# Attention units in four rounds in place of five, with both projections of the next unit at the front of the first round

## The chip, the cores and the metric

The kernel runs on one core of one Trainium2 chip. The metric is device time in microseconds (us). Before the change the median of three runs is 837.76 us (836.8 to 838.21).

## The reference, cut to what matters

The model is four residual blocks on x of shape (2, 1024, 128), in fp32: attention, a mixture of experts, a state space layer, and the mixture again. The change touches the attention alone:

```python
qk = layernorm(x) @ W_qk                    # 16 heads of 64, queries and keys
scores = (q * 64 ** -0.5) @ k.T, causal
out = softmax(scores) @ k                   # the keys are the values too
x = x + out @ W_out
```

Then come `x + ffn(layernorm(x))` (16 experts of width 64, the best 2, and a shared one), `x + ssm(layernorm(x))`, and the ffn again.

## The kernel before

Engines run programs of their own, written out by hand, and meet at semaphores. What each engine does next is fixed by the order of the calls in its program; no planner and no due times are involved. The attention is cut into 16 units, each one pair of heads (two heads of 64 rows, which fill 128 partitions) of one batch entry. For one unit:

- **K and Q** (`project`, L554 to L556): keys or queries of the unit, 2 halves x 3 matmuls of 512 columns into one ring buffer. Three matmuls per half because fp32 is carried as a high and a low part. ScalarE copies K out twice (L418 to `k_t`, L419 to `kh`) and Q once (L424 to `qh`); VectorE makes the low parts (`keys_low` L313, `queries_low` L480).
- **T** (`turn_keys`, L565): 16 small transposes that give the keys in natural order, copied out by ScalarE (L430).
- **M0 to M9** (`max_scores`, L578, causal mask L585): scores at high precision part only, for the row maxima; VectorE reduces each buffer (`maxima`, L487), then `join_maxima` (L494). TensorE turns the maxima round (`turn_max`, L595) and VectorE spreads them (`max_rows`, L499).
- **S0 to S8** (`scores`, L611, L613, L615, mask L618, maxima L620): the full scores, transposed; ScalarE takes the exponential of each buffer (`exponentials`, L448), GpSimd adds the probabilities up in 11 steps (`add_up`, L373, L380).
- **Outputs** (`outputs`, L638): probabilities times keys, fp32, in bursts; `denominators` (L651), logarithm and exponential on ScalarE (`invert`, L439, L441), and the product on VectorE (`scale_out`, L508), for each half of the queries.

K, Q, T, M and S all go through a ring of three PSUM buffers, each of two banks. A fill waits until the reader of the fill three places before it in the ring is done (`pair_free`): ScalarE's exponential for an S, VectorE's reduction for an M, the last copy for K, VectorE's `queries_low` for Q, ScalarE's copy for T. `ring_uses` lists the order of the fills; it has to be that of TensorE's program.

While unit u has its S fills, unit u+1 has its M fills and unit u-1 its outputs. `ROUNDS` gives the S and M fills of each round, `BURSTS` the slots of the output burst at the front of each round. TensorE's five rounds are, in order: round 0: turn_max(u), burst 0, T(u+1), S0, Q(u+1); round 1: burst 1, the denominators of the second half of u-1, S1 M0 S2 M1; round 2: burst 2 (one slot), S3 M2 S4 M3 M4; round 3: burst 3 (two slots), denominators of the first half of u, S5 M5 S6 M6 M7; round 4: burst 4, M8 S7 M9 S8, K(u+2). Bursts and denominators use 128 rows x 64 columns of the array (`128*64` in the trace), S, M and T use 64 rows (`64*128`), K and Q all of it (`128*128`).

On VectorE, round 0 of a unit holds `scale_out` of the first half of u-1 (it waits for burst 0), then `queries_low`, then the reductions.

Of the kernel before, what the change touches and what calls it, by code (L numbers as in the profile page):

```python
# [99 lines left out]
def layernorm_transposed(nc, s, k, load, banks, xn, sync_first, vector_first, gpsimd_work):  # L100
# [85 lines left out]
    def later(piece):  # L186
        def issue(eng):
# [7 lines left out]
UNITS = PAIRS * BATCH  # L195
# [9 lines left out]
NMAX = len(MAX_FILLS)  # L205

BURSTS = [[(0, 0), (1, 0), (2, 0), (1, 1)], [(3, 0), (2, 1)], [(4, 0)], [(5, 0), (6, 0)], [(7, 0), (8, 0), (8, 1)]]
NBURST = len(BURSTS)  # L210
ROUNDS = [[("S", 0)], [("S", 1), ("M", 0), ("S", 2), ("M", 1)], [("S", 3), ("M", 2), ("S", 4), ("M", 3), ("M", 4)],
          [("S", 5), ("M", 5), ("S", 6), ("M", 6), ("M", 7)], [("M", 8), ("S", 7), ("M", 9), ("S", 8)]]
FIRST_OF_HALF = {0: 0, 1: 1}
BURST_OF = [max(r for r, b in enumerate(BURSTS) if any(s == slot for s, _ in b)) for slot in range(NSLOT)]

# [6 lines left out]

def ring_uses():

    uses = [("K", 0, 0), ("Q", 0, 0), ("T", 0, 0)] + [("M", 0, m) for m in range(NMAX)] + [("K", 1, 0)]
    for unit in range(UNITS):
        more = unit + 1 < UNITS
        for r, row in enumerate(ROUNDS):
            if r == 0 and more:
                uses.append(("T", unit + 1, 0))  # L230
            uses += [(what, unit if what == "S" else unit + 1, n) for what, n in row if what == "S" or more]
            if r == 0 and more:
                uses.append(("Q", unit + 1, 0))
            if r == NBURST - 1 and unit + 2 < UNITS:
                uses.append(("K", unit + 2, 0))
    return uses


def attention(nc, k, w_qk, load_x, load_w_out):
    uses = ring_uses()  # L240
    number = {use: i for i, use in enumerate(uses)}

    with Scope(nc, "at") as s:
# [37 lines left out]
        def pair(what, unit, n=0):  # L281

            return ring[number[(what, unit, n)] % 3]
# [27 lines left out]
        def keys_low(eng, unit):  # L311
            eng.wait_ge(hi_done, 2 * unit + 1)
            eng.tensor_tensor(kl[unit % 2][:, :], k_t, kh[unit % 2][:, :].bitcast(FP32), ALU.subtract).then_inc(k_low, 1)  # L313
# [38 lines left out]
        with nc.Block() as block:  # L352
# [56 lines left out]
            @block.scalar  # L409
            def _(act):  # L410
                def keys_high(unit):

                    act.wait_ge(proj_ready, 2 * unit + 1)
                    if unit:
                        act.wait_ge(knat_ps_ready, unit)
                        act.wait_ge(k_low, unit)
                    bank = pair("K", unit)[:, :, :].rearrange("p h c -> p (h c)")
                    act.activation(k_t, bank, ACT.Copy).then_inc(kt_done, 1)  # L418
                    act.activation(kh[unit % 2][:, :], bank, ACT.Copy).then_inc(hi_done, 1)  # L419

                def queries_high(unit):
                    act.wait_ge(proj_ready, 2 * unit + 2)
                    bank = pair("Q", unit)[:, :, :].rearrange("p h c -> p (h c)")
                    act.activation(qh[unit % 2][:, :], bank, ACT.Copy).then_inc(hi_done, 1)  # L424

                def natural_keys(unit):

                    act.wait_ge(knat_ps_ready, unit + 1)
                    for l in range(2):
                        last = act.activation(k_nat[unit % 3][:, :, rows(l)],  # L430
                                              pair("T", unit)[:, l, :].rearrange("p (t c) -> p t c", t=QT), ACT.Copy)
                    last.then_inc(knat_done, 1)

                def invert(g, half):

                    n = 2 * g + half
                    act.wait_ge(den_ready, 2 * n + 2)
                    wait(act, out_used, n - 1)
                    act.activation(inv[half][:, :], misc[:, :], ACT.Ln).then_inc(ln_done, 1)  # L439
                    act.wait_ge(ln_done, n + 1)  # L440
                    act.activation(inv[half][:, :], inv[half][:, :], ACT.Exp, scale=-1.0).then_inc(inv_done, 1)  # L441

                def exponentials(unit, slot):
                    act.wait_ge(scores_ready, 2 * (NSLOT * unit + slot) + 2)
                    if unit:
                        act.wait_ge(av_done, 2 * (NBURST * (unit - 1) + BURST_OF[slot]) + 2)
                        act.wait_ge(summed, NSUM * (unit - 1) + SUMMED_AT[slot] + 1)
                    act.activation(probs[:, :, slot * BANK:(slot + 1) * BANK], pair("S", unit, slot)[:, :, :], ACT.Exp,  # L448
                                   scale=BETA).then_inc(exp_done, 1)

                act.preload_act_table_set("natural_log_exp_and_others")
                keys_high(0)
                queries_high(0)
                natural_keys(0)
                high_rest(act)
                keys_high(1)
                for unit in range(UNITS):
                    more = unit + 1 < UNITS
                    for r, row in enumerate(ROUNDS):
                        if r == 0 and more:  # L460
                            natural_keys(unit + 1)
                        if r == 1 and unit:
                            invert(unit - 1, 1)
                        if r == 3:
                            invert(unit, 0)
                        for what, slot in row:
                            if what == "S":
                                exponentials(unit, slot)
                        if r == 0 and more:
                            queries_high(unit + 1)  # L470
                        if r == NBURST - 1 and unit + 2 < UNITS:
                            keys_high(unit + 2)
                invert(UNITS - 1, 1)

            @block.vector
            def _(dve):
# [37 lines left out]
                        low_rest(dve)  # L514
                    maxima(0, m)
                join_maxima(0)
                keys_low(dve, 1)
                dve.wait_ge(consts, 9)
                for unit in range(UNITS):
                    more = unit + 1 < UNITS  # L520
                    for r, row in enumerate(ROUNDS):
                        if r == 0:
                            if unit == 0:
                                max_rows(0)
                            if unit:
                                scale_out(unit - 1, 0)
                            if more:
                                queries_low(unit + 1)
                        for what, m in row:
                            if what == "M" and more:  # L530
                                maxima(unit + 1, m)
                        if r == NBURST - 1:
                            if more:
                                join_maxima(unit + 1)
                            if unit:
                                scale_out(unit - 1, 1)
                            if more:
                                max_rows(unit + 1)
                            if unit + 2 < UNITS:
                                keys_low(dve, unit + 2)  # L540
                for half in range(2):
                    scale_out(UNITS - 1, half)

# [1 line left out]
            def _(pe):  # L545
# [115 lines left out]
                        turn_rest(pe)  # L661
                    max_scores(0, m)
                pe.wait_ge(x_low, GROUPS)
                project(1, "K")

                for unit in range(UNITS + 1):
                    more = unit + 1 < UNITS
                    for r, row in enumerate(ROUNDS):
                        if r == 0 and unit < UNITS:
                            turn_max(unit)  # L670
                        if unit:
                            outputs(unit - 1, r)
                        if r == 1 and unit:
                            denominators(unit - 1, 1)
                        if unit == UNITS:
                            continue
                        if r == 3:
                            denominators(unit, 0)
                        if r == 0 and more:
                            turn_keys(unit + 1)  # L680
                        for what, n in row:
                            if what == "S":
                                scores(unit, n)
                            elif more:
                                max_scores(unit + 1, n)
                        if r == 0 and more:
                            project(unit + 1, "Q")
                        if r == NBURST - 1 and unit + 2 < UNITS:
                            project(unit + 2, "K")


RING = 2
# [901 lines left out]
```

## Time and profile before

| | |
|---|---|
| median of three runs | 837.76 us |
| profiled execution | 837.44 us, its span 835.7 us |
| attention, first K(1) to last scale_out | about 34 to 506 us of the span |
| TensorE busy | 767.2 us, 92% |
| VectorE, ScalarE, GpSimd busy | 54%, 50%, 53% |
| mean granted TensorE clock | 0.965 |

TensorE's share of busy time is an average over the stages; what bounds the attention is read from a stretch of it. A matmul's duration in the trace is longer than the distance to the next one, since matmuls overlap in the pipeline: the distance between starts is what a matmul costs. An "x4" row merges instructions of one line that follow one another.

### The profile page before, as it was taken

The numbers are of one execution on the slowest core, as the hardware profiler recorded it, in microseconds if no ns is written. First come the engines' busy times: TensorE is split into PE (matmuls) and PEld (weight loads), VectorE is DVE, ScalarE is ACT, GpSimd is POOL, SyncE is SP. The second block draws the span as 40 slices with busy tenths as digits, with TensorE's granted clock in tenths as the row PEclk, the third lists the DMA queues.
The fourth block names the chain that finished last, engine by engine and source line by source line (L and its number), as shares of the span: only waits on it lengthen the run. The fifth ranks groups of instructions, "written<-read, shape, count | busy, mean of one in ns | idle before, by whom it ended". The sixth has DMA issues, their size and how long they took to land. (4 is left out here: it accounts for less than half of the span.)

```text
span 835.7 us, 15021 instructions
## 1 busy us (share of the span) xinstructions
PE 767.2 (92%) x6024; PEld 516.6 (62%) x6024; DVE 447.3 (54%) x856; ACT 422.0 (50%) x548; POOL 441.0 (53%) x320
## 2 busy tenths in 40 slices
PE   2699999999999999999999989999998856689998
PEld 2465655656565565656556548877887522667887
DVE  5755565556456555645655502655554775655442
ACT  2355545554554555455555442467555650376542
POOL 3266685666658557656855683143433453143443
PEclk9899999999999999999999999999999885899999
DMA  2000000000000000000000006100000000000000
GB/s 63 7 1 2 8 1 2 7 2 1 9 2 1 8 1 8 1 2 2 1 2 26 2 1 147 23 1 1 1 1 1 2 0 0 1 1 13 15 0 26
DMA packets 18964, 8.15 MB, mean 10 GB/s; under 512 B 7952, under 2 KB 18768, under 8 KB 18896
## 3 DMA queue, kind: packets, MB, share of 16 engines
q1 hardware_dynamic: 18896, 7.20, 3.3%
q8 instruction: 48, 0.79, 0.4%
q14 instruction: 20, 0.16, 0.1%
HBM read 6.15 MB, written 1.05 MB: 9 GB/s over the span
## 5 line engine op out<-in xcount | busy, mean ns | idle before, releaser
L373 POOL TENSOR_TENSOR all_x<-all_x,at_probs 128x1024 f32<-128x1024 f32 (+3 forms) x128 | 220.0, 1718 | 36.8 <-ACT at_probs L448 22.1
L487 DVE TENSOR_REDUCE at_half_max<-at_ring 128x2 f32<-128x1024 f32 (+1 forms) x192 | 177.2, 955 | 115.8 <-PE at_ring L585 101.9
L448 ACT ACTIVATE at_probs<-at_ring 128x1024 f32<-128x1024 f32 x144 | 147.2, 1023 | 123.4 <-PE at_ring L620 122.0
L1120 POOL TENSOR_TENSOR m_prod<-m_gate,m_wb_copy 128x512 f32<-128x512 f32 x64 | 82.0, 1286 | 115.8 <-ACT m_gate L957 113.3
L638 PE MATMUL at_out<-at_probs,at_k_nat 128*64 128x512 f32 (+3 forms) x768 | 140.3, 494 | 1.1 <-DVE a_attn_t L508 0.9
L373 POOL TENSOR_TENSOR all_x<-at_probs 128x768 f32<-128x768 f32 (+1 forms) x32 | 67.0, 2095 | 133.8 <-ACT at_probs L448 133.6
L638 PEld LDWEIGHTS at_out<-at_probs,at_k_nat 128*64 128x64 f32 x768 | 49.2, 136 | 68.2 <-issue 62.9
L1018 DVE TENSOR_TENSOR m_hid<-m_prod,m_u 128x512 f32<-128x512 f32 x64 | 43.9, 687 | 79.1 <-POOL m_prod L1120 69.6
L611 PE MATMUL at_ring<-at_qh,at_kh 64*128 64x512 f32 (+3 forms) x384 | 77.9, 402 | 3.0 <-DVE at_m_rows L499 2.6
L957 ACT ACTIVATE m_gate<-m_g 128x512 f32<-128x512 f32 x72 | 43.1, 599 | 73.6 <-PE m_g L846 73.3
L854 PEld LDWEIGHTS m_acc<-rest_wd,m_hid 128*128 128x128 f32 x576 | 74.7, 191 | 5.9
L620 PE MATMUL at_ring<-at_m_rows,at_ones_r 64*128 64x512 f32 (+3 forms) x384 | 76.1, 391 | 0.0
L854 PE MATMUL m_acc<-rest_wd,m_hid 128*128 128x128 f32 x576 | 75.1, 274 | 0.0
L578 PE MATMUL at_ring<-at_kh,at_qh 64*128 64x512 f32 (+3 forms) x384 | 67.9, 383 | 4.4 <-DVE at_half_max L487 2.8
L615 PE MATMUL at_ring<-at_qh,at_kl 64*128 64x512 f32 (+3 forms) x384 | 67.1, 345 | 0.0
L613 PE MATMUL at_ring<-at_ql,at_kh 64*128 64x512 f32 (+3 forms) x384 | 66.9, 344 | 0.0
L611 PEld LDWEIGHTS at_ring<-at_qh,at_kh 64*128 64x128 f32 x384 | 36.5, 187 | 41.7 <-issue 37.2
L578 PEld LDWEIGHTS at_ring<-at_kh,at_qh 64*128 64x128 f32 x384 | 38.6, 187 | 21.8 <-issue 19.7
L439 ACT ACTIVATE at_inv<-at_misc 128x512 f32<-128x512 f32 x32 | 19.1, 598 | 61.9 <-PE at_misc L651 61.9
L480 DVE TENSOR_TENSOR at_ql<-at_ring,at_qh 128x1024 fp32r<-128x1024 f32 x16 | 19.6, 1225 | 55.1 <-ACT at_qh L424 55.1
L948 ACT ACTIVATE m_wb_copy<-m_wb 128x512 f32<-128x512 f32 x64 | 38.0, 593 | 6.5 <-POOL m_prod L1120 3.4
L615 PEld LDWEIGHTS at_ring<-at_qh,at_kl 64*128 64x128 f32 x384 | 36.4, 186 | 4.2
(202 smaller groups left out, 1355.9 us busy)
## 6 DMA issues: line engine op xcount, KB each, us to landing
all_x<-in_L_attn_a_x SPq DMA_DIRECT2D x8, 256.0 KB, 4.0
at_w_raw<-in_L_attn_a_W_qk SPq DMA_DIRECT2D x8, 128.0 KB, 2.5
out<-all_x SPq DMA_DIRECT2D x4, 256.0 KB, 2.4
a_room<-in_L_attn_a_W_out SPq DMA_DIRECT2D x1, 512.0 KB, 4.5
m_raw_wg<-in_L_ffn_experts_wg SPq DMA_DIRECT2D x1, 512.0 KB, 4.9
m_raw_wu<-in_L_ffn_experts_wu SPq DMA_DIRECT2D x1, 512.0 KB, 4.1
rest_wd<-in_L_ffn_experts_wd SPq DMA_DIRECT2D x1, 512.0 KB, 4.2
rest_w_in<-in_L_attn_b_W_in SPq DMA_DIRECT2D x1, 256.0 KB, 4.2
```

The source lines that it names most:

```text
L373: return pool.tensor_tensor(sums[:, :, a * P:b * P], left, right, ALU.add)
L448: act.activation(probs[:, :, slot * BANK:(slot + 1) * BANK], pair("S", unit, slot)[:, :, :], ACT.Exp, scale=BETA).then_inc(exp_done, 1)
L487: last = dve.reduce_max(half_max[:, :, i, int(a > 0)], pair("M", unit, m)[:, :, at:at + (b - a) * P], AX.X)
L578: last = pe.matmul(out[:, l, at:at + (b - a) * P], qh[u][rows(l), i * P:(i + 1) * P], kh[u][rows(l), a * P:b * P], start=True, stop=not diag)
L611: pe.matmul(to[l], kh[u][rows(l), keys], qh[u][rows(l), q], start=True, stop=False)
L613: pe.matmul(to[l], kh[u][rows(l), keys], ql[u][rows(l), q], start=False, stop=False)
L615: pe.matmul(to[l], kl[u][rows(l), keys], qh[u][rows(l), q], start=False, stop=False)
L620: last = pe.matmul(to[l], ones_r[rows(l), :], m_rows[u][rows(l), q], start=False, stop=True)
L638: last = pe.matmul(out_ps[rows(l), o:o + (b - a) * P], k_nat[g % 3][:, j, rows(l)], probs[:, l, at:at + (b - a) * P], start=(j == 0), stop ...
L854: last = pe.matmul(acc[:, t * P:(t + 1) * P], hid[g % BUFS][:, t * P:(t + 1) * P], f.wd[:, st, :], start=(st == 0 and t == 0), stop=(st == ...
L1018: dve.tensor_tensor(hid[r][:, :], left[:, :], u_ps[g % RING][:, :], ALU.mult).then_inc(hid_ready, 1)
L1120: pool.tensor_tensor(prod[g % BUFS][:, :], gate[g % BUFS][:, :], wb[(LAST * n + st) % 2][:, :], ALU.mult)\
```

## The change

The round with one output slot is merged into the next: slots 4, 5 and 6 form one burst. The S and M fills are dealt over four rounds; S1 and M0 now follow S0 in round 0, and M9 follows S8 at the end. K and Q of the next unit are projected one behind the other at the front of round 0 (before, K was at the end of the unit before, and Q at the end of round 0). The copies on ScalarE move with them, ahead of T's copy, and `keys_low` goes behind `queries_low` on VectorE. `scale_out` stays ahead of `queries_low`. The first denominators of a unit are in the last round.

```diff
-BURSTS = [[(0, 0), (1, 0), (2, 0), (1, 1)], [(3, 0), (2, 1)], [(4, 0)], [(5, 0), (6, 0)], [(7, 0), (8, 0), (8, 1)]]
+BURSTS = [[(0, 0), (1, 0), (2, 0), (1, 1)], [(3, 0), (2, 1)], [(4, 0), (5, 0), (6, 0)], [(7, 0), (8, 0), (8, 1)]]
-ROUNDS = [[("S", 0)], [("S", 1), ("M", 0), ("S", 2), ("M", 1)], [("S", 3), ("M", 2), ("S", 4), ("M", 3), ("M", 4)],
-          [("S", 5), ("M", 5), ("S", 6), ("M", 6), ("M", 7)], [("M", 8), ("S", 7), ("M", 9), ("S", 8)]]
+ROUNDS = [[("S", 0), ("S", 1), ("M", 0)], [("S", 2), ("M", 1), ("S", 3), ("M", 2)],
+          [("S", 4), ("M", 3), ("S", 5), ("M", 4), ("S", 6), ("M", 5)],
+          [("M", 6), ("S", 7), ("M", 7), ("M", 8), ("S", 8), ("M", 9)]]
```

On ScalarE:

```diff
-                keys_high(1)
...
                         if r == 0 and more:
+                            keys_high(unit + 1)
+                            queries_high(unit + 1)
                             natural_keys(unit + 1)
...
-                        if r == 3:
+                        if r == NBURST - 1:
                             invert(unit, 0)
...
-                        if r == 0 and more:
-                            queries_high(unit + 1)
-                        if r == NBURST - 1 and unit + 2 < UNITS:
-                            keys_high(unit + 2)
```

On VectorE:

```diff
-                keys_low(dve, 1)
...
                                 scale_out(unit - 1, 0)
                             if more:
                                 queries_low(unit + 1)
+                                keys_low(dve, unit + 1)
...
-                            if unit + 2 < UNITS:
-                                keys_low(dve, unit + 2)
```

On TensorE:

```diff
-                project(1, "K")
...
+                        if r == 0 and more:
+                            project(unit + 1, "K")
+                            project(unit + 1, "Q")
                         if r == 0 and unit < UNITS:
                             turn_max(unit)
...
-                        if r == 3:
+                        if r == NBURST - 1:
                             denominators(unit, 0)
...
-                        if r == 0 and more:
-                            project(unit + 1, "Q")
-                        if r == NBURST - 1 and unit + 2 < UNITS:
-                            project(unit + 2, "K")
```

`ring_uses` changes to the same order.

## Rows read from the trace of the kernel before

**Rows 1.** The page, busy time of each engine over the span.
```profile
PE 767.2 (92%) x6024; PEld 516.6 (62%) x6024; DVE 447.3 (54%) x856; ACT 422.0 (50%) x548; POOL 441.0 (53%) x320
```
**Rows 2.** Stretches: start:end, length, busy us by engine, granted clock, DMA share, GB/s.
```profile
31.00:34.00 3.00, 2.50 (x19) 1.87 (x20) 3.00 (x5) 0.00 (x0) 0.00 (x0) 0.50 0.02 5
...
268.43:297.66 29.23, 29.23 (x277) 17.37 (x274) 16.19 (x18) 15.62 (x19) 19.53 (x13) 1.00 0.02 6
```
**Rows 3.** VectorE timeline, L499, once a unit (columns: start, duration, instruction, idle before).
```profile
93.28 1.22 DVE L499 TENSOR_TENSOR at_m_rows<-at_misc,at_neg_pick 128x1024 fp32r<-128x1024 f32 x1 [1.40 <-PE at_misc L595]
...
444.04 1.22 DVE L499 TENSOR_TENSOR at_m_rows<-at_misc,at_neg_pick 128x1024 fp32r<-128x1024 f32 x1 [1.40 <-PE at_misc L595]
```
**Rows 4.** TensorE timeline of one unit, from T over S0 and Q to burst 1.
```profile
270.68 0.71 PE L565 MATMUL at_ring<-all_ident,a_room 64*128 64x64 f32 x16
...
272.07 0.50 PE L620 MATMUL at_ring<-at_m_rows,at_ones_r 64*128 64x512 f32 x2
272.50 0.50 PE L554 MATMUL at_ring<-all_xhi,at_w_hi 128*128 128x512 f32 x1
272.84 0.40 PE L555 MATMUL at_ring<-all_xlo,at_w_hi 128*128 128x512 f32 x1
...
273.76 0.40 PE L556 MATMUL at_ring<-all_xhi,at_w_lo 128*128 128x512 f32 x1
274.09 1.51 PE L638 MATMUL at_out<-at_probs,at_k_nat 128*64 128x512 f32 x8
```
**Rows 5.** TensorE timeline of the same unit, parts of rounds 2, 3 and 4.
```profile
282.08 0.40 PE L620 MATMUL at_ring<-at_m_rows,at_ones_r 64*128 64x512 f32 x2
...
283.38 0.40 PE L620 MATMUL at_ring<-at_m_rows,at_ones_r 64*128 64x512 f32 x2
283.72 0.73 PE L578 MATMUL at_ring<-at_kh,at_qh 64*128 64x512 f32 x4
...
289.19 0.40 PE L620 MATMUL at_ring<-at_m_rows,at_ones_r 64*128 64x512 f32 x2
289.57 0.73 PE L578 MATMUL at_ring<-at_kh,at_qh 64*128 64x512 f32 x4
290.23 1.94 PE L638 MATMUL at_out<-at_probs,at_k_nat 128*64 128x512 f32 x12
...
293.55 0.48 PE L620 MATMUL at_ring<-at_m_rows,at_ones_r 64*128 64x512 f32 x2
293.87 0.40 PE L578 MATMUL at_ring<-at_kh,at_qh 64*128 64x512 f32 x2
```
**Rows 6.** ScalarE timeline, the exponential of S3.
```profile
282.55 1.02 ACT L448 ACTIVATE at_probs<-at_ring 128x1024 f32<-128x1024 f32 x1 [1.49 <-PE at_ring L620]
```
**Rows 7.** VectorE timeline, reductions of M3 and M4.
```profile
284.26 2.36 DVE L487 TENSOR_REDUCE at_half_max<-at_ring 128x2 f32<-128x1024 f32 x2 [0.45 <-PE at_ring L578]
```
**Rows 8.** Unit 0, TensorE: S0, Q(1), S1, S2.
```profile
40.98 0.71 PE L611 MATMUL at_ring<-at_qh,at_kh 64*128 64x512 f32 x2 [2.60 <-DVE at_m_rows L499]
...
43.24 0.79 PE L554 MATMUL at_ring<-all_xhi,at_w_hi 128*128 128x512 f32 x1
...
45.40 0.44 PE L611 MATMUL at_ring<-at_qh,at_kh 64*128 64x384 f32 x2
...
47.84 0.39 PE L611 MATMUL at_ring<-at_qh,at_kh 64*128 64x256 f32 x2 [0.23 <-DVE at_ql L480]
```
**Rows 9.** Unit 0, VectorE: queries_low.
```profile
46.56 1.22 DVE L480 TENSOR_TENSOR at_ql<-at_ring,at_qh 128x1024 fp32r<-128x1024 f32 x1 [5.64 <-ACT at_qh L424]
```
**Rows 10.** Unit 15, TensorE: S0 behind burst 0.
```profile
474.29 0.50 PE L611 MATMUL at_ring<-at_qh,at_kh 64*128 64x512 f32 x2
```
**Rows 11.** Unit 15, VectorE: scale_out behind burst 0.
```profile
474.47 0.69 DVE L508 TENSOR_TENSOR a_attn_t<-at_out,at_inv 128x512 f32<-128x512 f32 x1 [1.40 <-PE at_out L638]
```
**Rows 12.** Unit 15, GpSimd: the sum steps 4 to 10.
```profile
485.56 2.38 POOL L373 TENSOR_TENSOR all_x<-at_probs 128x1024 f32<-128x1024 f32 x1 [0.17 <-POOL all_x L373]
488.08 11.64 POOL L373 TENSOR_TENSOR all_x<-all_x,at_probs 128x512 f32<-128x512 f32 x6
```

More of the change, by code:

```diff
@@ L223, in ring_uses @@
 def ring_uses():
-    uses = [("K", 0, 0), ("Q", 0, 0), ("T", 0, 0)] + [("M", 0, m) for m in range(NMAX)] + [("K", 1, 0)]
+    uses = [("K", 0, 0), ("Q", 0, 0), ("T", 0, 0)] + [("M", 0, m) for m in range(NMAX)]
     for unit in range(UNITS):
         more = unit + 1 < UNITS
-        for r, row in enumerate(ROUNDS):
-            if r == 0 and more:
-                uses.append(("T", unit + 1, 0))
+        if more:
+            uses += [("K", unit + 1, 0), ("Q", unit + 1, 0), ("T", unit + 1, 0)]
+        for row in ROUNDS:
             uses += [(what, unit if what == "S" else unit + 1, n) for what, n in row if what == "S" or more]
-            if r == 0 and more:
-                uses.append(("Q", unit + 1, 0))
-            if r == NBURST - 1 and unit + 2 < UNITS:
-                uses.append(("K", unit + 2, 0))
     return uses
@@ L468, in _ @@
                                 exponentials(unit, slot)
-                        if r == 0 and more:
-                            queries_high(unit + 1)
-                        if r == NBURST - 1 and unit + 2 < UNITS:
-                            keys_high(unit + 2)
                 invert(UNITS - 1, 1)
@@ L685, in _ @@
                                 max_scores(unit + 1, n)
-                        if r == 0 and more:
-                            project(unit + 1, "Q")
-                        if r == NBURST - 1 and unit + 2 < UNITS:
-                            project(unit + 2, "K")
 RING = 2
```

## The prediction

> **What bounds the kernel now.** First the page: TensorE is busy 92% of the span, the others 50 to 54% [rows 1]. Then a stretch of exactly one unit: TensorE busy for 29.23 of 29.23 us at a granted clock of 1.00, GpSimd next with 19.53, VectorE 16.19, ScalarE 15.62 [rows 2]. So the attention goes at TensorE's pace. The row that each unit has once gives the period: (444.04 - 93.28) / 12 = 29.23 us [rows 3]. A change of 0.1 us in that period moves the total by 1.4 us, for 14 units (1 to 14) repeat the pattern. Busy time doesn't say whether the array streams, so I then read the starts in TensorE's timeline. From 272.84 to 273.76 four fills of 512 columns start 0.23 us apart [rows 4]. Any larger distance between such fills is a switch or a wait, and the change trades the one for the other.
>
> **What the change removes**, per unit:
>
> - The burst of one slot. Going into a burst costs 0.20: M6 and M7 start at 289.57, the burst at 290.23, 0.66 for two fills of 0.23 [rows 5]. Coming out costs 0.10 + 0.11: the distance from Q's last matmul to the next kind of work is 0.33 in place of 0.23 (273.76 to 274.09), and the first fill after a change of kind takes 0.34 (272.50 to 272.84) [rows 4]. Sum 0.41.
> - Q between S0 and burst 1: S0's last fill to Q 0.43 (272.07 to 272.50) [rows 4], where a score fill goes on to the next ring fill in 0.32 (293.55 to 293.87) [rows 5]; Q's first fill 0.11; Q to burst 0.10. Against it M0 to burst 1 costs 0.11 more than M0 to S2 did (half of the 0.20 above, M0 ends in a mask). Net 0.21.
> - An S fill behind a causal mask starts with the same 0.09 (0.32 - 0.23). Five S fills stand behind a masked M before, two after: 0.27.
> - Two waits on the ring: 283.38 to 283.72 is 0.34, so 0.11 too long, and 289.19 to 289.57 is 0.38, 0.15 too long [rows 5]. Both are an M fill that finds the S of three places before still being read: 0.26.
>
> Sum 1.15 us a unit. With nothing else the period would be 28.08.
>
> **What it adds** are waits on the ring. Two durations set them. An S: last fill at 282.08 [rows 5], exponential from 282.55 for 1.02 to 283.57 [rows 6], the fill that waited for it at 283.72 [rows 5]. So an S buffer is free 1.41 us after the end of the fill (282.08 + 0.23). An M: fills at 283.72 [rows 5], reduction at 284.26, two of them in 2.36, so 1.23 for one and 1.14 for the next [rows 7]. From the end of the fill (283.95) that is 0.31 + 1.23 and the hand-back to TensorE, which is 0.06 where a fill waited for VectorE (46.56 + 1.22 = 47.78, fill at 47.84) [rows 8, 9]: 1.60. Between a fill and the third after it stand two others; an S costs about 0.93 and an unmasked M 0.23, 1.16 together, less than 1.41 or 1.60. Before, a burst of 1 to 2 us came every four or five fills and paid the rest. Six fills in a row don't have that cover.
>
> - Round 2, from S4's start: S4 ends at 1.04, M3 1.27, S5 2.20; M4 wants S4's buffer, free at 2.45 (wait 0.25), ends 2.68; S6 wants M3's, free at 2.87 (wait 0.19, and 0.05 for the restart); M5 wants S5's, free at 3.61, no wait. 0.49.
> - Round 3, from M6's start: M6 ends 0.34, S7 1.45, M7 1.68; M8 wants M6's buffer, free at 1.94: 0.26 (and 0.05); it ends 2.51; S8 wants S7's, free at 2.86: 0.35. M9 wants M7's, free at about 3.1: none. 0.66. ScalarE's `invert` of 1.2 us ends before S7 is full.
> - Round 0, S1. It takes Q's buffer, and so waits for `queries_low`. On VectorE this is queued behind `scale_out`, which waits for burst 0. Call the start of T t. Burst 0 to `scale_out`: in unit 15 S0 follows the burst at 474.29 with 0.05 for the switch, and `scale_out` starts at 474.47 [rows 10, 11], so t + 0.23; 0.59 until the next instruction starts (0.69 less the 0.10 by which VectorE's instructions overlap); `queries_low` 1.22 [rows 9]; hand-back 0.06: t + 2.10. TensorE is there at 1.40 (270.68 to S0's last fill 272.07 [rows 4]) + 0.32 = t + 1.72. Wait 0.38, restart 0.08: 0.46. Before, the same low part had S1, M0 and burst 1 with its denominators as cover. Behind the waiting S1 stand M0 and burst 1, so all of it counts.
> - Round 1: M2 wants S2's buffer: 0.03.
>
> Without cost: `turn_max` has K and Q, 3.0 us, for the reduction of M9, which needs 0.3 + 1.2 + 0.2. Q takes S8's buffer with K's 1.5 us as cover. M0 takes T's, with S0, S1. ScalarE's three copies for K and Q (3 x 1.0) end before T's is wanted. GpSimd's sums end some 6 us before the denominators, even if they start 2 us later. DMA (0.02 of a unit's time [rows 2]) is not touched, and SP's queue keeps its order.
>
> Added per unit 1.64, removed 1.15: period 29.72, +0.49. Bounds: with no wait at all -1.15; with each wait twice as long +2.1. I take 0.49, since each wait is built from durations of the same instructions.
>
> **The ends.** Unit 0: Q(1) stood between S0 and S1, 45.40 - 43.24 = 2.16 [rows 8]. Now it runs while TensorE waited anyway: S0 sat 2.60 idle for `max_rows` [rows 8], and `turn_max` moves only as far as `keys_low` on VectorE moves behind. S0 stays at about 41. -2.2 (bounds -3.5 and -0.5: half clock there).
> Unit 14 to 15: no K or Q covers M9's reduction, `join_maxima` and their hand-backs. `turn_max` waits about 1.5 in place of 0.2: +1.3 once.
> Unit 15: GpSimd goes without a break from step 4 of the sums, 485.56, to 488.08 + 11.64 = 499.72 [rows 12], and the last denominators wait for it. From S0 (474.29) step 4 starts at 11.3. After the change S4 stands behind a burst of three slots: S0, S1 to 2.6, burst 1 and denominators to 5.0, S2, S3 to 7.4, burst 2 to 10.2, S4 to 11.2, its exponential to 12.5. Step 4 at 12.6: +1.3 (bounds 0 and 2).
>
> **Sum** against the profiled execution: 14 x 0.49 = 6.9, -2.2, +1.3, +1.3: +7.3. Its time is 837.44 with a span of 835.7; the median of the runs is 0.3 above it. 837.4 + 7.3 = 844.7; the later waits in unit 0 (rounds with no bursts at all, before and after) come out slightly in favour of the new order, so I say 844.
>
> **Rivals.**
>
> 1. The switches decide and the waits are hidden: the period is 28.08, 14 x -1.15 = -16.1, -2.2, +2.6: 822. For it: TensorE is the bound, and every removed switch is in its timeline. Against it: two of the waits are there before already, at the places where cover is thinnest, and a queue of six fills in three buffers must show them. It decides from the point where the added waits are under 1.18 a unit (-0.5 from the ends): then the change is no loss.
> The Trainium skill ("TensorEngine Tiling (Array Packing)", Key Properties) says that a change of tiling mode drains TensorE. The trace agrees, 0.1 to 0.2 us at each change [rows 4, 5]; by that rule alone fewer bursts make the kernel faster, and its time would be rival 1's.
> 2. Half of it: one of the three places (S1, or a round) has more cover than I give it, say VectorE runs `scale_out` earlier or the buffers come free 0.15 sooner. Added 1.2, period 29.25: 838.
> 3. The clock falls. In 31 to 34, behind idle pieces of TensorE, the granted clock is 0.50, the lower level (1.2 GHz) [rows 2]. If the short waits of rounds 2 and 3 did that once a unit, the 4 us of a round's fills would take some 2 us more: 14 x 2 = 28, 872. Against: the unit from 268.43 has two such waits and stays at 1.00 [rows 2].
> The Trainium skill ("TensorE: Matmul & The Clock Gate", A second HAM failure mode: psum-queue depth-cycling) tells of a clock that oscillates when TensorE idles briefly between groups of matmuls. So far the trace doesn't bear it out for waits of 0.11 and 0.15; no row shows one of 0.5 in a steady unit.
> 4. The waits compound (S1 late, then the reductions bunch up): period 30.2, 851.
>
> **Chances.** Forecast (840 to 849) 0.52, rival 1 0.14, rival 2 0.18, rival 3 0.04, rival 4 0.12. What a measurement can tell from no change is 0.2%, 1.7 us. Rival 2 is half in that band and a quarter to each side; so faster 0.19, same 0.12, slower 0.69. The range for 8 in 10 is 832 to 853: part of rival 1 and all of rival 3 are outside.
>
> **What would show it.** The row of L499 [rows 3] repeats every 29.7 us. S1's first fill (L611) starts 2.1 after T's first transpose, and is put down to L480. In round 2 the third and fifth distance between fills, and in round 3 M8 and S8, are longer by 0.2 to 0.35, put down to L448 and L487. L638 comes in four bursts. S1 of unit 0 starts near 43, the sum step 4 of unit 15 starts 12.6 after S0. A period of 28.1 would make me wrong on the waits; a clock under 1.00 between 60 and 490 would be rival 3.

## The result, and the profile after

The changed kernel takes 845.9 us (median of 6 runs, 844.08 to 846.2), before 838.24 (6 runs): ratio 1.0090, 95% interval 1.0077 to 1.0103. It is slower, by 0.9%. The forecast was 844, with a range of 832 to 853. The profiled execution took 844.08 us with a span of 842.3, so its span is 6.6 us over that of before. It is the fastest of the six and 1.8 under their median; what is read from the trace below explains its own +6.6, and the rest of the +7.7 between the medians has no trace.

First the page of the changed kernel, busy times as in [rows 1]:

```profile
PE 768.2 (91%) x6024; PEld 521.1 (62%) x6024; DVE 446.0 (53%) x856; ACT 422.4 (50%) x548; POOL 428.9 (51%) x320
```

TensorE has the same 6024 matmuls and 1 us more of busy time in a span 6.6 us longer: what was added is mostly idle time. VectorE's timeline, the row that each unit has once, answers to [rows 3]:

```profile
59.82 1.22 DVE L494 TENSOR_TENSOR at_m_rows<-at_misc,at_neg_pick 128x1024 fp32r<-128x1024 f32 x1 [1.93 <-PE at_misc L588]
...
447.25 1.23 DVE L494 TENSOR_TENSOR at_m_rows<-at_misc,at_neg_pick 128x1024 fp32r<-128x1024 f32 x1 [1.33 <-PE at_misc L588]
```

(447.25 - 59.82) / 13 = 29.80 us a unit in place of 29.23. The granted clock of a long stretch is unchanged, and TensorE has idle time in it where a unit had none before [rows 2]:

```profile
60.00:490.00 430.00, 422.10 (x3918) 253.65 (x3916) 228.40 (x254) 222.44 (x257) 259.30 (x173) 1.00 0.02 4
```

The view of waits of the same stretch names three of them (columns: engine, line, waited for, us in total, times, longest; PEld is the load of the weights ahead of a matmul). In the same view of before, no row of TensorE that comes 14 times names VectorE or ScalarE:

```profile
PE at_ring L604 <- DVE at_ql L475: 2.9, 14, 0.2
PE at_misc L588 <- DVE at_row_max L489: 1.6, 1, 1.6
...
PEld at_ring L604 <- DVE at_ql L475: 7.3, 14, 0.5
...
PEld at_ring L604 <- ACT at_probs L446: 3.3, 14, 0.2
...
PEld at_ring L604 <- DVE at_half_max L482: 2.2, 14, 0.2
```

Once a unit the first score matmul of a fill (L604) waits for the low queries (S1), once for an exponential (S8), once for a reduction (S6). The waits of M4 and M8 (L571) have no row of their own and are read from the starts. The single 1.6 is `turn_max` of unit 15. In TensorE's timeline of one unit most of the places are seen: T, then S1; then of the round of six S4's first matmuls, S5's last, M4, S6 and the burst behind it; then M6 and S8 of the last round, and K.

```profile
270.46 0.71 PE L558 MATMUL at_ring<-all_ident,a_room 64*128 64x64 f32 x16
...
272.55 0.44 PE L604 MATMUL at_ring<-at_qh,at_kh 64*128 64x384 f32 x2 [0.21 <-DVE at_ql L475]
...
283.03 0.50 PE L604 MATMUL at_ring<-at_qh,at_kh 64*128 64x512 f32 x2
...
284.99 0.40 PE L613 MATMUL at_ring<-at_m_rows,at_ones_r 64*128 64x512 f32 x2
285.47 0.49 PE L571 MATMUL at_ring<-at_kh,at_qh 64*128 64x512 f32 x2
285.81 0.50 PE L604 MATMUL at_ring<-at_qh,at_kh 64*128 64x512 f32 x2
...
287.23 1.94 PE L631 MATMUL at_out<-at_probs,at_k_nat 128*64 128x512 f32 x12
...
289.97 0.50 PE L571 MATMUL at_ring<-at_kh,at_qh 64*128 64x512 f32 x2
...
292.73 0.44 PE L604 MATMUL at_ring<-at_qh,at_kh 64*128 64x384 f32 x2
...
294.74 0.50 PE L547 MATMUL at_ring<-all_xhi,at_w_hi 128*128 128x512 f32 x1
```

S1 starts at T + 2.09. M4 starts 0.48 after S5's last matmuls (285.47 - 284.99), where 0.23 is the distance without a wait. VectorE's rows of the same stretch show why S1 is late: `scale_out` at 270.67, right behind burst 0, and the low queries only behind it:

```profile
270.67 0.69 DVE L503 TENSOR_TENSOR a_attn_t<-at_out,at_inv 128x512 f32<-128x512 f32 x1 [1.00 <-PE at_out L631]
271.28 1.21 DVE L475 TENSOR_TENSOR at_ql<-at_ring,at_qh 128x1024 fp32r<-128x1024 f32 x1
```

The end of the attention, TensorE and GpSimd. These answer to [rows 10, 12]:

```profile
475.19 0.44 PE L588 MATMUL at_misc<-all_ident,at_row_max 128*64 128x128 f32 x4 [1.57 <-DVE at_row_max L489]
...
478.14 0.50 PE L604 MATMUL at_ring<-at_qh,at_kh 64*128 64x512 f32 x2
...
504.88 1.89 PE L644 MATMUL at_misc<-all_x,at_ones 128*64 128x512 f32 x4 [3.35 <-POOL all_x L371]
506.55 5.40 PE L631 MATMUL at_out<-at_probs,at_k_nat 128*64 128x512 f32 x24
```

```profile
490.69 2.37 POOL L371 TENSOR_TENSOR all_x<-at_probs 128x1024 f32<-128x1024 f32 x1 [3.52 <-ACT at_probs L446]
493.20 11.62 POOL L371 TENSOR_TENSOR all_x<-all_x,at_probs 128x512 f32<-128x512 f32 x6
```

The sum of the profiled executions, to the last `scale_out` of the attention (505.30 before, 512.10 after, +6.8):

| stretch | before | after | difference |
|---|---|---|---|
| to K(2), end of unit 0 | 61.93 | 56.31 | -5.6 |
| 13 units | 29.23 each | 29.80 each | +7.4 |
| K(15) to S0 of unit 15 | 32.4 | 34.4 | +2.0 |
| S0 of unit 15 to the last scale_out | 31.0 | 34.0 | +3.0 |

0.5 of the -5.6 has nothing to do with the change: TensorE reaches the first K(1) at 33.66 before and at 33.16 after, and everything that was changed comes behind that.

### The profile page after: what moved, and what is told of

It is laid out like the page before. It is cut to its first block and busy times, and to the rows that moved or that the text cites. A ratio compares the mean times of both kernels' runs of the same rounds, so it can differ in the third digit from the quotient of the medians.

```text
span 842.3 us, 15021 instructions
## 1 busy us (share of the span) xinstructions
PE 768.2 (91%) x6024; PEld 521.1 (62%) x6024; DVE 446.0 (53%) x856; ACT 422.4 (50%) x548; POOL 428.9 (51%) x320
## 5 line engine op out<-in xcount | busy, mean ns | idle before, releaser
L482 DVE TENSOR_REDUCE at_half_max<-at_ring 128x2 f32<-128x1024 f32 (+1 forms) x192 | 179.0, 957 | 161.8 <-PE at_ring L571 79.6
L371 POOL TENSOR_TENSOR all_x<-all_x,at_probs 128x1024 f32<-128x1024 f32 (+3 forms) x128 | 207.7, 1622 | 32.9 <-ACT at_probs L446 16.3
L631 PE MATMUL at_out<-at_probs,at_k_nat 128*64 128x512 f32 (+3 forms) x768 | 137.9, 495 | 1.1 <-DVE a_attn_t L503 0.9
L631 PEld LDWEIGHTS at_out<-at_probs,at_k_nat 128*64 128x64 f32 x768 | 51.0, 137 | 68.4 <-issue 60.3
L571 PE MATMUL at_ring<-at_kh,at_qh 64*128 64x512 f32 (+3 forms) x384 | 75.0, 393 | 6.5 <-DVE at_half_max L482 2.8
L604 PE MATMUL at_ring<-at_qh,at_kh 64*128 64x512 f32 (+3 forms) x384 | 75.5, 390 | 4.5 <-DVE at_ql L475 2.9
L571 PEld LDWEIGHTS at_ring<-at_kh,at_qh 64*128 64x128 f32 x384 | 38.9, 188 | 38.3 <-issue 36.7
L604 PEld LDWEIGHTS at_ring<-at_qh,at_kh 64*128 64x128 f32 x384 | 36.4, 186 | 40.3 <-issue 25.3
L503 DVE TENSOR_TENSOR a_attn_t<-at_out,at_inv 128x512 f32<-128x512 f32 x32 | 22.0, 687 | 47.1 <-PE at_out L631 47.1
```

Source lines behind the costliest of these rows:

```text
L371: return pool.tensor_tensor(sums[:, :, a * P:b * P], left, right, ALU.add)
L482: last = dve.reduce_max(half_max[:, :, i, int(a > 0)], pair("M", unit, m)[:, :, at:at + (b - a) * P], AX.X)
L571: last = pe.matmul(out[:, l, at:at + (b - a) * P], qh[u][rows(l), i * P:(i + 1) * P], kh[u][rows(l), a * P:b * P], start=True, stop=not diag)
L604: pe.matmul(to[l], kh[u][rows(l), keys], qh[u][rows(l), q], start=True, stop=False)
L631: last = pe.matmul(out_ps[rows(l), o:o + (b - a) * P], k_nat[g % 3][:, j, rows(l)], probs[:, l, at:at + (b - a) * P], start=(j == 0), stop ...
```

## The experiments

Each experiment ran beside the kernel before on one chip; the ratio is to that. The period is read as above, from VectorE's `max_rows` rows.

**1. The low queries ahead of scale_out** (`low_first`), one order swapped on VectorE:

```diff
+                            if more:
+                                queries_low(unit + 1)
                             if unit:
                                 scale_out(unit - 1, 0)
                             if more:
-                                queries_low(unit + 1)
                                 keys_low(dve, unit + 1)
```

> The changed kernel with one order swapped on VectorE: in round 0 the low part of the next queries is made ahead of scale_out, so it no longer waits for burst 0. Theory W (the loss is waits on the ring, 0.46 us a unit of it at S1): S1 starts 1.7 us after T in place of 2.09, the period of a unit falls from 29.80 to 29.34, and the total by 14 x 0.46 = 6.4 us, to 839.5 (ratio to before 1.0015). Nothing waits for the later scale_out: burst 1 starts some 4 us behind it. Rival A (the wait at S1 only stands for a later one, TensorE is held again by the next reader): period stays at 29.7 to 29.8, 845 to 846 us. Rival B (the loss is the place of the projections, by the copies on ScalarE): no change either, and S2 or M0 waits in place of S1.

Measured: 838.02 us (11 runs), ratio 0.9999 (0.9990 to 1.0009). VectorE's rows:

```profile
89.90 1.23 DVE L494 TENSOR_TENSOR at_m_rows<-at_misc,at_neg_pick 128x1024 fp32r<-128x1024 f32 x1 [1.33 <-PE at_misc L589]
...
441.74 1.23 DVE L494 TENSOR_TENSOR at_m_rows<-at_misc,at_neg_pick 128x1024 fp32r<-128x1024 f32 x1 [1.32 <-PE at_misc L589]
```

Period (441.74 - 89.90) / 12 = 29.32, as theory W has it. Its view of waits keeps the rows of an exponential (3.2 us, 14 times) and of a reduction (2.2, 14), and the one of `at_ql` is gone. 0.48 us of the unit's added time was this wait. Rivals A and B are out. The total is 1.5 us under the 839.5 expected, which the period doesn't explain.

**2. Five rounds, projections in front** (`five_front`): `BURSTS`, `ROUNDS` and the round of the first denominators as before, the rest of the change kept.

> The changed kernel with the rounds and bursts of before: only K and Q of the next unit stay together at the front of round 0. Theory W: burst 1 and the denominators stand between S0 and S1 again and cover the low part of the queries, rounds have at most five fills, so only the two old waits of 0.11 and 0.15 are left, and Q's own switch (0.21) is saved: period 29.02, 14 x -0.21 = -2.9, and unit 0 gains its 2 to 5 us: 831 to 834 us, ratio 0.991 to 0.995. Rival B (putting the projections together is itself the loss, as ScalarE has three copies in a row ahead of the next exponentials): period 29.5 or more, total over 838.

Measured: 830.86 us (5 runs), ratio 0.9916 (0.9903 to 0.9930); period (439.96 - 91.49) / 12 = 29.04. The total is 0.1 under the range expected. So the one half of the change is a gain of 0.9%, and the other half lost that and 0.9% more. Rival B is out for good.

**3. The merged burst taken apart** (`split_burst`):

```diff
-BURSTS = [..., [(4, 0), (5, 0), (6, 0)], [(7, 0), (8, 0), (8, 1)]]
+BURSTS = [..., [(4, 0)], [(5, 0), (6, 0)], [(7, 0), (8, 0), (8, 1)]]
-          [("S", 4), ("M", 3), ("S", 5), ("M", 4), ("S", 6), ("M", 5)],
+          [("S", 4), ("M", 3), ("S", 5)], [("M", 4), ("S", 6), ("M", 5)],
```

> The changed kernel with the merged burst taken apart again: slot 4 alone ahead of S4 M3 S5, slots 5 and 6 ahead of M4 S6 M5; rounds 0, 1 and the last as in the changed kernel. Theory W: the two waits of the six fills (0.49) go and one more switch in and out comes (0.41): period 29.7 (29.6 to 29.8), so the merge was worth nothing in the steady state. In the last unit GpSimd's step 4 starts 1.7 us earlier behind S0, which gives 1.3 at the end. Total 843 to 845.5. Rival C (the merge itself is the loss, beyond its waits): period 29.3 or less, 839. Rival D (the merge is a gain, the loss all in round 0 and the last round): period 30.1, 849.

Measured: 844.94 us (5 runs), ratio 1.0078 (1.0064 to 1.0092); period (449.86 - 91.06) / 12 = 29.90. The total fits theory W, the period is 0.2 over its 29.7. ScalarE's timeline has the reason: S5 is filled ahead of the burst that frees its place in the probabilities, so its exponential waits for that burst, and M5 for the exponential.

```profile
287.67 1.03 ACT L446 ACTIVATE at_probs<-at_ring 128x1024 f32<-128x1024 f32 x1 [2.06 <-PE at_out L631]
```

That wait was my own addition, so the experiment doesn't say to 0.1 us what a split is worth. M5 starts 0.31 after the matmuls before it (288.53 to 288.84) and is itself some 0.1 longer, so the addition is worth about 0.2 and the period without it would be near 29.7. That excludes rival C (29.3) and rival D (30.1).

**4. All reads short, after and before.** Every exponential and reduction of maxima on half of its columns; `after_short` has the order of experiment 1 too. Not shown are the constant that is written to the probabilities once, ahead of the attention, and the waits for it.

```diff
-    last = dve.reduce_max(..., pair("M", unit, m)[:, :, at:at + (b - a) * P], AX.X)
+    last = dve.reduce_max(..., pair("M", unit, m)[:, :, at:at + (b - a) * P // 2], AX.X)
-    act.activation(probs[:, :, slot * BANK:(slot + 1) * BANK], pair("S", unit, slot)[:, :, :], ...)
+    act.activation(probs[:, :, slot * BANK:slot * BANK + BANK // 2], pair("S", unit, slot)[:, :, 0:BANK // 2], ...)
```

> The order of the changed kernel with the low part of the queries first, and every exponential and every reduction of maxima cut to half of its columns (the rest of the probabilities is a constant, the maxima are those of half of the keys). The fills on TensorE are the same. Theory W: a buffer of S is free 1.0 us after its fill in place of 1.41, one of M about 1.05 in place of 1.60, both under the 1.16 of the two fills between, so no fill waits, and the period is the sum of the fills and switches: 28.1 us. Rival E (the array itself takes longer in the new order, the waits are a small part): 28.6 or more. Its total also has a constant written ahead of the attention, so only its period is read.

> The kernel before with every exponential and every reduction of maxima cut to half of its columns (the rest of the probabilities is a constant, the maxima are those of half of the keys). Theory W: its two waits (0.11 and 0.15) go, period 29.23 - 0.26 = 28.97, 0.7 above the same cut of the changed order (28.26 measured), as the switches say. Rival E (the switches are worth nothing, the short kernel is faster for another reason): under 28.5. Only the period is read.

VectorE's rows, first of `after_short`, then of `before_short`:

```profile
91.18 1.23 DVE L497 TENSOR_TENSOR at_m_rows<-at_misc,at_neg_pick 128x1024 fp32r<-128x1024 f32 x1 [1.86 <-PE at_misc L592]
...
430.32 1.23 DVE L497 TENSOR_TENSOR at_m_rows<-at_misc,at_neg_pick 128x1024 fp32r<-128x1024 f32 x1 [1.86 <-PE at_misc L592]
```

```profile
95.86 1.23 DVE L502 TENSOR_TENSOR at_m_rows<-at_misc,at_neg_pick 128x1024 fp32r<-128x1024 f32 x1 [1.91 <-PE at_misc L598]
...
440.90 1.22 DVE L502 TENSOR_TENSOR at_m_rows<-at_misc,at_neg_pick 128x1024 fp32r<-128x1024 f32 x1 [1.91 <-PE at_misc L598]
```

Periods 28.26 and 28.75 (totals 825.06 and 832.1 us, one run each; the two do less work, and only their periods are read). In `after_short` one wait is left, S8's (PEld row `<- ACT at_probs`, 2.4 us in 14 times, 0.17 each), so the fills and switches of the new order come to about 28.1, and rival E is out. `before_short` is 0.22 under its expectation: the two old waits cost 29.23 - 28.75 = 0.48, not 0.26. Its timeline shows the rest. With no wait ahead of them, M3 and M4 take 0.56 to the burst behind, where [rows 5] has 0.66 for M6 and M7: a fill that waited is also followed at 0.33 to 0.34 in place of 0.23 (S6 of the changed kernel waits, starts at 285.81 and is followed at 286.14). A wait costs its length and a restart of 0.1. Shorter reads also free ScalarE and VectorE, so this pair alone doesn't separate the two; experiment 7 comes back to it.

**5. Only the reductions short, after** (`after_short_max`).

> The changed kernel with only the reductions of maxima cut to half of their columns (the maxima are those of half of the keys); exponentials whole, scale_out ahead of the low queries as in the change. Theory W, step by step on the ring: S6 no longer waits for M3 (-0.24 with its restart) and M8 not for M6 (-0.26), but S8 behind M8 wants S7's buffer, which comes free at the same time as ever, so the 0.26 comes back there, and only the restart of M8 (0.05) stays: period 29.80 - 0.29 = 29.5. Rival G (the waits simply add up by their reader, all those on VectorE go): 29.80 - 0.55 = 29.25. The low queries' wait of S1 stays in both.

Measured: 837.38 (one run), period (440.88 - 84.58) / 12 = 29.69. Neither number: the gain is 0.11. From M6 to S8 it takes 284.15 to 286.90, 2.75 us, and in the changed kernel 289.97 to 292.73, 2.76: as theory W has it, S8 wants an exponential that ends when it ended before, and whatever a shorter reduction gives at M8 is waited for again there. In round 2 less came than expected, since M4's own restart already covered most of S6's wait (S6 starts 0.31 after M4, 279.76 to 280.07, in place of 0.34).

**6. Four rounds, projections where they were** (`four_old_proj`): the new `BURSTS` and `ROUNDS` in the kernel before, Q right behind S0.

> The kernel before with the four rounds and bursts of the changed kernel, and the projections where they were: K at the end of the unit before, Q right behind S0. Theory W: against the changed kernel the wait of S1 for the low queries goes (-0.46, T's buffer is what S1 takes, and burst 1 covers the low part), Q has its own switch again (+0.21), the waits of rounds 2 and 3 stay: period 29.55 (29.5 to 29.65), so 0.3 over the kernel before. Unit 0 gains nothing, since Q stands behind S0; the end loses what the changed kernel loses there (M9 last, sum step 4 later, about 3 to 4 us with the clock). Total 838.2 + 14 x 0.33 + 3.5 = 846, 844 to 848. Rival F (rounds of six fills cost only together with the projections at the front): period 29.2 to 29.3, 842 or less.

Measured: 854.7 us (5 runs), ratio 1.0198 (1.0185 to 1.0212); period (486.36 - 94.01) / 13 = 30.18, 0.6 over what I expected; the total is 8.7 over the 846 expected, and 14 x 0.63 of it is 8.8. The view of waits, TensorE:

```profile
PEld at_misc L598 <- DVE at_row_max L497: 7.5, 15, 1.7
...
PE at_out L641 <- issue: 2.9, 14, 0.2
```

With M9 last, `join_maxima` and `scale_out` of the second half end late, and K alone doesn't cover them: burst 0 starts 0.64 after `turn_max` (275.23 against 274.59) in place of 0.27. From K to T it takes 4.59 (272.95 to 277.54), where `low_first` takes 4.12 without the 1.40 of its Q. The other 0.39 of the 0.86 between their periods is Q's own place, where I had put 0.21: the 0.21 was worked out for a Q that goes over into a burst, and here S1 follows, at 0.33 and with first matmuls of 0.28. So Q behind K isn't only a saved switch, it is the cover for M9 at the end of the unit. The two halves of the change don't add up: front projections alone -0.19 a unit, four rounds alone +0.95, both +0.57.

**7. Other orders of the M fills.** Same work. `five_mixed` is `five_front` with `MAX_FILLS` permuted; `four_mixed` is the changed kernel with `MAX_FILLS` permuted, the low queries first as in experiment 1, four fills in round 0 and five in the last.

`five_mixed` has the doubly masked fills second in rounds 2 and 3 (M2 and M5), between two S fills:

```diff
+MAX_FILLS = [[(2, 0, 3, 0)], [(3, 0, 4, 0)], [(0, 0, 1, 0), (1, 0, 2, P)], [(4, 0, 4, 0)], [(5, 0, 4, 0)], [(4, 4, 5, 0), (5, 4, 6, P)], [(6, 0, 4, 0)], [(7, 0, 4, 0)], [(6, 4, 7, 0)], [(7, 4, 8, 0)]]
```

`four_mixed`:

```diff
+MAX_FILLS = [[(4, 0, 4, 0)], [(5, 0, 4, 0)], [(0, 0, 1, 0), (1, 0, 2, P)], [(2, 0, 3, 0)], [(4, 4, 5, 0), (5, 4, 6, P)], [(3, 0, 4, 0)], [(6, 4, 7, 0)], [(6, 0, 4, 0)], [(7, 4, 8, 0)], [(7, 0, 4, 0)]]
+ROUNDS = [[("S", 0), ("S", 1), ("M", 0), ("M", 1)], [("S", 2), ("M", 2), ("S", 3), ("M", 3)],
+          [("S", 4), ("M", 4), ("S", 5), ("M", 5), ("S", 6), ("M", 6)],
+          [("M", 7), ("S", 7), ("M", 8), ("S", 8), ("M", 9)]]
```

> The five-round kernel with both projections in front, and the M fills dealt in another order: the two fills with two masked blocks (0.52 and 0.57 us on TensorE) stand third last in rounds 2 and 3, in the place of those of 0.27, so S, M and S between an S and the fill that takes its buffer come to over 1.41. Same work. Theory W: M3 and M6 wait no more; halving the reads showed that the two old waits cost 0.48 a unit with their restarts, so the period falls from 29.04 to 28.56 and the total from 830.9 by 14 x 0.48 = 6.7 to 824 (822 to 826). Rival H (the short reads were faster for another reason than the waits, as they also free ScalarE and VectorE): the named 0.26 at most, 28.8 to 29.0, 827 to 830.

> The four rounds of the change with the low queries first, and M fills dealt anew: two unmasked ones in round 0 behind S1, the two doubly masked ones between the S fills of rounds 1 and 2, five fills in the last round in place of six. Same work, four bursts. Theory W: every fill finds its buffer nearly free, waits of 0.1 to 0.3 a unit left, period 28.2 to 28.4 (29.80 in the changed kernel, 29.32 with the low queries first). The end keeps what the four rounds lose there (M9 or its like last before turn_max, sum step 4 later, clock). Total 838.0 - 14 x 1.0 = 824, 822 to 827, about the same as the five rounds. Rival C (four rounds have a cost that no order of fills takes away): period 28.9 or more, 832.

`five_mixed`: 830.86 us (4 runs), ratio 0.9912 (0.9895 to 0.9928), period (440.75 - 91.42) / 12 = 29.11. No gain, against my expectation. M3 indeed starts 0.23 after S4's last fill (0.35 in `five_front`), but then M3 and M4 take 0.85 to the burst in place of 0.66. M4 takes the buffer of the doubly masked fill, and VectorE's timeline has its two reductions until 278.63 + 1.02 = 279.65, where M4 would have streamed on at 279.62:

```profile
278.63 1.02 DVE L480 TENSOR_REDUCE at_half_max<-at_ring 128x2 f32<-128x256 f32 x2 [1.40 <-PE at_ring L576]
```

The wait moved on by one fill and from ScalarE to VectorE, and it is longer than the 0.03 between these two numbers. The weights of M4 are loaded at 279.78, and its matmuls start at 279.81 (TensorE's timeline up to 279.80 has two matmuls of L569, up to 279.82 four):

```profile
279.78 0.21 PEld L569 LDWEIGHTS at_ring<-at_kh,at_qh 64*128 64x128 f32 x2 [0.28 <-issue]
```

So the wait is 0.19, and from M4 to the burst it takes 0.43 (279.81 to 280.24) where it takes 0.33 without a wait: 0.19 and a restart of 0.10 are the 0.29 that M3 and M4 take over `before_short`. Of the 0.19, the hand-back is 0.16 (279.65 to 279.81), where 0.06 had been read off an S fill. Rival H isn't shown by it, since a wait is there to be seen: I had left out a reader.

`four_mixed`: 827.07 us (4 runs), ratio 0.9871 (0.9854 to 0.9887), the fastest with the whole work, and 0.07 above the range that I gave. VectorE's rows:

```profile
88.39 1.23 DVE L493 TENSOR_TENSOR at_m_rows<-at_misc,at_neg_pick 128x1024 fp32r<-128x1024 f32 x1 [1.32 <-PE at_misc L588]
...
429.89 1.23 DVE L493 TENSOR_TENSOR at_m_rows<-at_misc,at_neg_pick 128x1024 fp32r<-128x1024 f32 x1 [1.32 <-PE at_misc L588]
```

Period 28.46, also 0.06 above its range. Rival C (28.9 or more) is out: within a unit, four rounds have no such cost of their own. It is how the fills were dealt to them, and the low queries behind `scale_out`, that cost.

## Why the prediction was right

By its own steps, with the periods 28.75 (before, no wait), 28.1 (after, no wait), 29.32 (experiment 1):

- Removed, 1.15 a unit. Measured 29.23 - 28.1 = 1.13 to 1.17. The sum held, its parts did not: 0.48 of it were the two old waits (put at 0.26), some 0.65 to 0.7 the switches and masks (put at 0.89). The 0.20 into a burst was read off a place where a waiting fill stood ahead [rows 5], so half of it was the restart. That is 0.1 of the difference; the rest isn't traced to a row.
- Added, 1.64 a unit. Measured 29.80 - 28.1 = 1.7. S1: 0.48 (0.46 said), shown by experiment 1 and by T + 2.09 (2.10 said). Round 2 from S4 to its burst: 4.20 in the changed kernel (283.03 to 287.23), 3.74 in `after_short` (274.68 to 278.42), so 0.46 (0.49). Last round from M6 to K: 4.77 (289.97 to 294.74) and 4.35 (281.15 to 285.50), with 0.1 to 0.2 of S8's wait still in the short kernel: nearly 0.6 (0.66). Round 1: 0.17 where I had 0.03. M2's short wait drags a restart (its first matmuls take 0.26, 279.81 to 280.07, where 0.18 is usual for 384 columns); this is most of what the period was over the forecast (+0.57 against +0.49).
- Two errors in the latencies cancelled. M8 waited 0.26 as said (291.42 for M7, 291.91 for M8, by the timeline cut there), but VectorE began on M6 0.09 sooner than worked out, and the hand-back was 0.15 in place of 0.06. For S8 nothing cancelled: it started 2.76 after M6 and not 2.86, since S7's buffer came back 1.31 after the end of the fill and not 1.41. The hand-back goes with the fill that waits, not with the engine that read (last section).
- Unit 0: said -2.2 (bounds -3.5 and -0.5), measured -5.1 from K(1) on. Mis-sized, and outside the bounds. S0 started at 39.91 and S1 at 41.13, where about 41 and 43 were said. From K(1) to S0 it took 0.6 less, from S0 to S1 3.2 less (2.16 of Q, the rest the clock, below), and from S1 to K(2) 1.35 less, with fewer waits.
- Unit 14 to 15: said +1.3, `turn_max` waited 1.57 as said (1.5); with one more period's 0.57 this is the +2.0 of the table.
- Unit 15: step 4 of the sums started at 490.69 - 478.14 = 12.55 behind S0 (12.6 said), and the last denominators 26.74 behind S0 in place of 25.49: +1.25 (+1.3 said, bounds 0 and 2). The stretch lost 3.0, though: 1.7 more came behind the denominators, with the clock.

The mechanism and the size of the added waits held. The total is in part luck: unit 0 gave 2.9 more than said and the start 0.5, the tail and the 0.08 a unit took 2.8, so errors of opposite signs cancelled. Rival 1 (switches decide) fails by the waits that TensorE's view shows, rival 2 by each of the three places being as long as worked out. Rival 3 is out within the units: granted clock 1.00 from 60 to 490. Its price was low besides: at the lower level the last denominators took 1.81 to 1.98 in place of 1.08, so 4 us of fills would have cost over 3 us more a unit, not 2.

The Trainium skill ("TensorEngine Tiling (Array Packing)", Key Properties) has a change of mode drain TensorE. The trace agrees, and its price here is about 0.1 us at each side of a burst and 0.1 for the first fill behind it. By that rule alone the change would have been a gain. It is outdone because the burst was also the time in which ScalarE and VectorE emptied the ring.

## What to carry to other kernels

In a program where fills go through a ring of three buffers, count for each fill what the two fills before it cost on TensorE, against the latency of the reader of the third (1.3 to 1.4 us for an exponential, 1.5 to 1.6 for a reduction here). A stretch of other work between the fills (a burst, a projection) is cover, and removing a switch removes cover. Before merging rounds, look whether long and short fills can be dealt so that cover isn't needed: here the low queries first took +0.9% to 0.0%, and the fills dealt anew took that to -1.3%, with the same work. And don't judge the two halves of a change together: one half was worth -0.9% alone.

## What the runs showed of the hardware

The granted clock at the two ends of the attention moved with TensorE's idle time. Before, TensorE idled 2.60 us ahead of S0 in unit 0 [rows 8] and got the lower level (1.2 GHz) behind it; after, Q filled part of that place, the idle ahead of S0 was 0.78, and the clock stayed at the higher level (2.4 GHz). The same columns as in [rows 2], before and after:

```profile
42.00:44.00 2.00, 2.00 (x12) 1.13 (x9) 0.00 (x0) 0.63 (x1) 0.00 (x0) 0.50 0.00 0
```

```profile
42.00:44.00 2.00, 2.00 (x42) 1.92 (x42) 0.80 (x3) 1.42 (x2) 0.11 (x1) 1.00 0.00 0
```

At the end it went the other way, before and after:

```profile
506.00:508.00 2.00, 1.68 (x15) 1.72 (x16) 0.00 (x0) 1.28 (x1) 1.73 (x3) 1.00 0.14 38
```

```profile
506.00:508.00 2.00, 2.00 (x6) 0.49 (x4) 0.00 (x0) 1.13 (x2) 0.00 (x0) 0.50 0.00 0
```

The last denominators waited for GpSimd 3.35, 3.33, 3.36 and 3.34 us in the changed kernel, `low_first`, `four_mixed` and `four_old_proj`; all four ran the matmuls behind it at half clock, 1.81 to 1.98 us for the denominators in place of 1.08. In the kernel before, `five_front`, `five_mixed` and `split_burst` the wait was 1.67, 1.69, 1.68 and 1.27, and the clock stayed. So GpSimd's 1.3 us cost 3.0 in all.

A wait's length alone doesn't decide it. `turn_max` of unit 15 waits 1.57 us in the changed kernel, `low_first`, `split_burst`, `four_mixed` and `four_old_proj`. Behind it, burst 0 took 2.38 us in the first two, at a granted clock of 1.00, and 3.67, 3.81 and 4.01 us in the other three, where the clock had fallen to 0.50. First the changed kernel, then `split_burst`:

```profile
475.84 2.38 PE L631 MATMUL at_out<-at_probs,at_k_nat 128*64 128x512 f32 x16 [0.20 <-issue]
```

```profile
478.54 3.67 PE L631 MATMUL at_out<-at_probs,at_k_nat 128*64 128x512 f32 x16 [0.21 <-issue]
```

So the totals of these three have 1.3 to 1.6 us in them that their periods don't, and differences of 1 to 2 us between totals say nothing about a unit. Whether the clock falls in every execution of a kernel no run shows; each was profiled once.

The hand-back, from the end of the reader to the first matmul of the fill that waited for it, goes with the fill. An S fill starts 0.05 us behind either engine (272.55 behind the low queries, which end at 271.28 + 1.21; S8 at 292.73 behind an exponential that ends at 291.65 + 1.02), an M fill 0.14 to 0.15 behind either (M4 at 285.47 behind 284.30 + 1.02; M8 at 291.91 behind 290.53 + 1.23). It is the same in the other units of the changed kernel and of `low_first`. In the program, an M fill waits for two semaphores ahead of its first matmul, an S fill other than S0 for one; whether that is the 0.1 us is likely, but not tested.
